# Two half-filled weight blocks share one: the feed-forward stage of a layer with 16-head attention

## The reference

```
xn  = layernorm(x)                          # x: 2048 tokens x 256
att = softmax(q k^T / sqrt(128)) v          # 16 heads of 128, q, k, v from xn @ Wqkv.T
x1  = xn @ quant(w1).T                      # quant(w): each weight to -1, 0 or 1
x2  = xn @ quant(w2).T                      # 704 inner features
ffn = (sigmoid(x1) * x2) @ quant(w3).T      # 704 -> 256
out = x + att @ Wout.T + ffn
```

## Time and profile before

| | before |
|---|---|
| median of 3 runs | 1920.66 us (1920.07 to 1921.25) |
| the profiled execution | 1918.09 us |
| its span, first to last instruction | 1916.3 us |
| PE busy | 1873.7 us, 98% of the span, 9540 matmuls |
| DVE, POOL, ACT busy | 1648.0, 1352.1, 1253.9 us |
| mean granted PE clock | 0.996 of full |

### The profile page before, as it was taken

One profiled execution on the slowest core, in us unless ns is written; L12 is line 12 of the kernel. 1 busy time (PEld: TensorE's weight loads), 2 busy tenths in 40 slices (PEclk: granted clock), 3 DMA queues, 4 the chain that ended last, 5 costly groups with the idle time before them and its releaser, 6 DMA issues.

```text
span 1916.3 us, 29455 instructions
## 1 busy us (share of the span) xinstructions
PE 1873.7 (98%) x9540; PEld 1583.2 (83%) x9540; DVE 1648.0 (86%) x2216; ACT 1253.9 (65%) x1700; POOL 1352.1 (71%) x514
## 2 busy tenths in 40 slices
PE   5979999999999999999999999999999999999998
PEld 4868888888888888888888888888888888888887
DVE  6368898898989889898989989898998989889895
ACT  3437676766767676666767666676766667666664
POOL 2418687776868777686877768687776868777685
PEclk9999999999999999999999999999999999999999
DMA  3037677676767767676776767677676767767664
GB/s 106 0 81 174 156 171 171 156 170 158 173 156 173 172 151 172 158 170 157 174 170 152 171 158 170 158 173 171 152 170 158 169 159 170 174 147 168 156 159 128
DMA packets 195827, 298.59 MB, mean 156 GB/s; under 512 B 37888, under 2 KB 57024, under 8 KB 195776
## 3 DMA queue, kind: packets, MB, share of 16 engines
q1 hardware_dynamic: 195776, 298.01, 66.5%
HBM read 12.65 MB, written 2.10 MB: 8 GB/s over the span
## 4 chain that ended last, share of the span: by engine, by line
PE 90%; DVE 3%; SPq 2%; POOL 2%; ACT 1%; issue 1%; DMA 1%; DVEq 0%; POOLq 0%; ACTq 0%
PE ps_o L375 23%; PE ps_o L377 12%; PE ps_s L367 11%; PE ps_s L369 11%; PE ps_s L368 11%; PE ps_s L338 5%; PE ps_t L357 4%; PE ps_t L347 4%; SPq L284 2%; PE ps_s L410 2%; PE ps_o L385 1%; PE ps_o L387 1%; PE ps_o L386 1%; POOL parts L1044 1%; DVE prob L896 1%
## 5 line engine op out<-in xcount | busy, mean ns | idle before, releaser
L1044 POOL TENSOR_TENSOR parts<-raw,parts 128x2048 fp32r<-128x2048 f32 x254 | 1176.8, 4634 | 446.0 <-ACT parts L674 445.1
L686 ACT ACTIVATE prob<-ps_s,neg_max 128x1024 f32<-128x1024 f32 x512 | 567.4, 1115 | 470.9 <-DVE neg_max L890 470.9
L375 PE MATMUL ps_o<-parts,v_hi 128*128 128x512 f32 x2032 | 728.7, 397 | 2.6 <-POOL v_lo L1037 2.6
L886 DVE TENSOR_REDUCE row_max<-ps_s 128x1 f32<-128x1024 f32 x512 | 612.2, 1213 | 68.8 <-PE ps_s L369 49.5
L896 DVE STREAM_TRANSPOSE prob<-prob 128x1024 f32<-128x1024 f32 x508 | 599.5, 1218 | 57.6 <-ACT prob L686 57.2
L377 PE MATMUL ps_o<-parts,v_lo 128*128 128x256 f32 x2032 | 571.2, 281 | 0.0
L674 ACT CAST parts<-raw 128x2048 fp32r<-128x2048 f32 x254 | 486.7, 1916 | 87.9 <-DMA raw<-prob 86.7
L375 PEld LDWEIGHTS ps_o<-parts,v_hi 128*128 128x128 f32 x2032 | 382.3, 188 | 91.3 <-issue 3.9
L367 PE MATMUL ps_s<-k_hi,q_hi 128*128 128x512 f32 x1024 | 404.7, 395 | 11.6 <-ACT prob L686 11.0
L369 PE MATMUL ps_s<-k_hi,q_lo 128*128 128x512 f32 x1024 | 400.8, 391 | 0.0
L368 PE MATMUL ps_s<-k_lo,q_hi 128*128 128x512 f32 x1024 | 400.3, 391 | 0.0
(11 more groups left out here) (113 smaller groups left out, 1630.2 us busy)
## 6 DMA issues: line engine op xcount, KB each, us to landing
raw<-prob SPq DMA_DIRECT2D x2032, 128.0 KB, 2.4
v_raw<-v_turned SPq DMA_DIRECT2D x244, 64.0 KB, 2.0
w_raw<-wqkv_dram SPq DMA_DIRECT2D x32, 128.0 KB, 2.5
y<-x_dram SPq DMA_DIRECT2D x4, 512.0 KB, 6.0
wo_raw<-wqkv_dram SPq DMA_DIRECT2D x16, 128.0 KB, 2.5
wo_raw<-wo_dram SPq DMA_DIRECT2D x16, 128.0 KB, 2.3
out_dram<-y SPq DMA_DIRECT2D x8, 256.0 KB, 2.7
w_raw<-w_dram SPq DMA_DIRECT2D x2, 704.0 KB, 10.6
```

The source lines that it names most:

```text
L375: nc.tensor.matmul(ps_pv, v_hi[:, kb, :], parts[:, kb].rearrange("p s a q -> p (s a q)"), start=(kb == 0), stop=False, skip_group_check=True)
L686: nc.scalar.activation(tile, logit, ACT.Exp, bias=neg_max[:, t:t + 1], scale=SCALE, accum_out=row_sum[:, t, half:half + 1]).then_inc(s_exp, 1)
L886: nc.vector.reduce_max(row_max[:, t, half:half + 1], ps_s[:, 2 * half:2 * half + 2, :].rearrange("p b n -> p (b n)"), AX_X).then_inc(s_mx, 1)
L1044: nc.gpsimd.tensor_tensor(half_of(0, half), moved(p, half), half_of(1, half), ALU.subtract).then_inc(s_pl, 1)
```

## The change

The last block of w1 (64 columns) and the last block of w2 (64 columns) are put into one block of `w1_q`. One set of 4 matmuls then gives x1's last 64 features on partitions 0 to 63 and x2's on 64 to 127 of one bank. ACT's sigmoid reads partitions 0 to 63 and writes 64 to 127, and DVE multiplies there. The high part stays on partitions 64 to 127 of `hid_hi`'s last block; the low part is now made by DVE and written to partitions 0 to 63 of the same block, and POOL's loop has five blocks. The last 64 rows of w3 are loaded a second time, beneath the first copy, so that one matmul for each tile multiplies high and low part together. The second load overwrites the zeros that the mean of w3 needs, and waits for that mean.

```diff
             w1_q = sb("w1_q", [P, C, FB * P], F32R, early)
-            w2_q = sb("w2_q", [P, C, FB * P], F32R, early)
+            w2_q = sb("w2_q", [P, C, FL], F32R, early)
...
-            hid_lo = sb("hid_lo", [P, FB, CH], F32R, early)
+            hid_lo = sb("hid_lo", [P, FB - 1, CH], F32R, early)
...
                 load_part(part, 0)
+            sp.wait_ge(s_abs, 3)
+            sp.dma_start(w3_raw[FR:P, FB - 1, :], w3_d[FL:FF, :]).then_inc(s_w3_again, 16)
...
-                for w, k in ((w1_q, 0), (w2_q, 1)):
+                for w, k in ((w1_q, 0), (w2_q, 1))[:1 if b == FB - 1 else 2]:
...
             def ffn_down(g):
                 for b in range(FB):
-                    pe.wait_ge(s_hidl, g * FB + b + 1)
+                    if b < FB - 1:
+                        pe.wait_ge(s_hidl, g * (FB - 1) + b + 1)
+                    else:
+                        pe.wait_ge(s_hidlast, g + 1)
                     for j in range(TG):
                         dst = (ps_t if j < 2 else ps_o)[:, j % 2, 0:DIM]
-                        nc.tensor.matmul(dst, hid_hi[:, b, j * P:(j + 1) * P], w3_q[:, b, :],
-                                         start=(b == 0), stop=False)
-                        last = nc.tensor.matmul(dst, hid_lo[:, b, j * P:(j + 1) * P], w3_q[:, b, :],
-                                                start=False, stop=(b == FB - 1))
+                        last = nc.tensor.matmul(dst, hid_hi[:, b, j * P:(j + 1) * P], w3_q[:, b, :],
+                                                start=(b == 0), stop=(b == FB - 1))
+                        if b < FB - 1:
+                            nc.tensor.matmul(dst, hid_lo[:, b, j * P:(j + 1) * P], w3_q[:, b, :],
+                                             start=False, stop=False)
...
             for b in range(FB):
+                if b == FB - 1:
+                    pe.wait_ge(s_wshared, 1)
                 ffn_up(0, b, b == 0)
...
-                nc.scalar.activation(sig[:, b % 2, :], ps_s[:, 2 * (b % 2), :], ACT.Sigmoid).then_inc(s_sig, 1)
+                n = FR if b == FB - 1 else P
+                nc.scalar.activation(sig[P - n:P, b % 2, :], ps_s[0:n, 2 * (b % 2), :], ACT.Sigmoid
+                                     ).then_inc(s_sig, 1)
...
-                nc.scalar.copy(hid_hi[:, b, :], hid[:, b % 2, :]).then_inc(s_hidh, 1)
+                n = FR if b == FB - 1 else P
+                nc.scalar.copy(hid_hi[P - n:P, b, :], hid[P - n:P, b % 2, :]).then_inc(s_hidh, 1)
...
-            quantise(1, w2_raw, w2_q[:, :, 0:FF])
+            quantise(1, w2_raw, w2_q[:], w1_q[:, :, FF:FB * P])
...
-                    dve.wait_ge(s_hidl, g * FB + b - 1)
-                nc.vector.tensor_tensor(hid[:, b % 2, :], ps_s[:, 2 * (b % 2) + 1, :], sig[:, b % 2, :],
+                    dve.wait_ge(s_hidl, g * (FB - 1) + b - 1)
+                n, bank = (FR, 2 * (b % 2)) if b == FB - 1 else (P, 2 * (b % 2) + 1)
+                nc.vector.tensor_tensor(hid[P - n:P, b % 2, :], ps_s[P - n:P, bank, :], sig[P - n:P, b % 2, :],
                                         ALU.mult).then_inc(s_hid, 1)
...
             def add_ffn(g):
+                dve.wait_ge(s_hidh, g * FB + FB)
+                nc.vector.tensor_tensor(hid_hi[0:FR, FB - 1, :], hid[FR:P, (FB - 1) % 2, :], hid_hi[FR:P, FB - 1, :],
+                                        ALU.subtract).then_inc(s_hidlast, 1)
                 dve.wait_ge(s_down, g + 1)
...
                     dve.wait_ge(s_gamma, 6)
+                    dve.wait_ge(s_w3_again, 16)
                     quantise(2, w3_raw, w3_q[:])
...
-            nc.gpsimd.memset(w1_q[:, :, FF:FB * P].bitcast(F32), 0.0).then_inc(s_pads, 1)
-            nc.gpsimd.memset(w2_q[:, :, FF:FB * P].bitcast(F32), 0.0).then_inc(s_pads, 1)
...
-                for b in range(FB):
+                for b in range(FB - 1):
```

More of the change, by code:

```diff
@@ L39 @@
 FR = FF - (FB - 1) * P
+FL = FF - FR
 G = 4
@@ L191, in build @@
         s_wq = sem("quantised_weights_ready")
+        s_wshared = sem("shared_block_ready")
+        s_w3_again = sem("w3_last_rows_loaded_again")
         s_ln = sem("layernorm_step_done")
@@ L202, in build @@
         s_hidl = sem("hidden_low_ready")
+        s_hidlast = sem("hidden_last_low_ready")
         s_down = sem("ffn_down_done")
@@ L815, in thresholds, with quantise @@
                                         ).then_inc(s_gamma, 1)
-            def quantise(i, raw, q):
+            def quantise(i, raw, q, shared=None):
                 n = raw.shape[1] * raw.shape[2]
@@ L821, in quantise @@
                     dve.wait_ge(s_wq, i)
+                if i == 2:
+                    dve.wait_ge(s_wshared, 1)
                 nc.vector.tensor_scalar(is_below, raw[:], half_gamma[:, 1, i:i + 1], None, ALU.is_lt
@@ L824, in quantise @@
                 dve.wait_ge(s_below, i + 1)
-                nc.vector.scalar_tensor_tensor(out=q, in0=raw[:], scalar=half_gamma[:, 0, i:i + 1], in1=is_below,
-                                               op0=ALU.is_gt, op1=ALU.subtract).then_inc(s_wq, 1)
+                n = raw.shape[2] if shared is None else FL
+                nc.vector.scalar_tensor_tensor(out=q, in0=raw[:, :, 0:n], scalar=half_gamma[:, 0, i:i + 1],
+                                               in1=is_below[:, :, 0:n], op0=ALU.is_gt, op1=ALU.subtract
+                                               ).then_inc(s_wq, 1)
+                if shared is not None:
+                    nc.vector.scalar_tensor_tensor(out=shared, in0=raw[:, :, FL:FF],
+                                                   scalar=half_gamma[:, 0, i:i + 1], in1=is_below[:, :, FL:FF],
+                                                   op0=ALU.is_gt, op1=ALU.subtract).then_inc(s_wshared, 1)
             normalise(0)
@@ L1004, in _ @@
             nc.gpsimd.memset(ident[:], 0.0).then_inc(s_pads, 1)
-            nc.gpsimd.memset(w1_q[:, :, FF:FB * P].bitcast(F32), 0.0).then_inc(s_pads, 1)
-            nc.gpsimd.memset(w2_q[:, :, FF:FB * P].bitcast(F32), 0.0).then_inc(s_pads, 1)
-            pool.wait_ge(s_pads, 3)
+            pool.wait_ge(s_pads, 1)
             nc.gpsimd.memset(w3_raw[FR:P, FB - 1, :], 0.0).then_inc(s_w3_pad, 1)
@@ L1010, in _ @@
             nc.gpsimd.memset(ones[:], 1.0).then_inc(s_pads, 1)
-            pool.wait_ge(s_pads, 4)
+            pool.wait_ge(s_pads, 2)
             nc.gpsimd.affine_select(out=ident[:], in_=ident[:], compare_op=ALU.not_equal, fill=1.0, base=0,
```

## The result

| | before | changed |
|---|---|---|
| median of 6 runs each, on the same chip | 1919.3 us (1917.29 to 1921.25) | 1912.47 us (1910.85 to 1915.14) |
| ratio, 95% interval | | 0.9966 (0.9954 to 0.9978) |
| the profiled execution | 1918.09 us | 1913.44 us |

A forecast was written before the change was run, and what follows sets the result against it. PE, busy for 98% of the span, was taken to bound the kernel. Removed work, added instructions and clock, -4.66 + 0.19 + 0.3 = -4.2 us, off the median 1920.66 gave 1916.5 us, range 1914.7 to 1918.2.

The forecast's parts named there:

- Groups 1 to 3: Feed-forward groups without PE waits: each loses 4 up and 4 down matmuls, 1.39 us, 4.18 us for three.
- The up matmuls of group 0: Ahead of the wait for w3: their 0.92 us gain nothing, PE waits 3.3 us instead of 2.4.
- The sixth block: Last block of the down-projection: its low part from DVE arrives in time, margin 0.8 us, so no cost.
- DVE's second instruction: Quantising w2 becomes two DVE instructions; the normalising behind starts some 0.06 us later, and that goes on the path.
- The clock, +0.3 us: Group 0's down-projection behind the w3 wait: longer idle brings more of the lower clock rate, 0.3 us lost.
- rival B: Group 0's first 11 down matmuls run slow too, costing 1.03 us: gain 3.4 us, 1917.2 us; chance 0.20.
- The registers, +0.13 us: Down-projection loop on PE: 12 more register and sequencer instructions over three groups, 0.011 us each, 0.13 us added.
- The attention is left as it is and only begins earlier: The over 1800 us behind the feed-forward stage: unchanged in length, only starting earlier.
- heads of a changed length: Attention: heads whose length has changed would show the forecast wrong; no size given.
- The level: Whole kernel: the 4.2 us gain taken off the runs' median, 1920.66 us, 2.6 us above the profiled execution: 1916.5 us.
- C: Group 0's slow clock stretch vanishes or falls into the gap: gain 6.0 us, 1914.7 us; chance 0.12.
- rival E: Sixth down block: moving between partition halves makes the serial chain 2.5 times as long, 5.7 us slower, 1926.4 us; chance 0.03.

The follow-up runs named there:

- the down part alone: Kernel before with only the down-projection's last block shared, 4 matmuls in place of 8, up-weights in separate zero-padded blocks; 1914.88 us, ratio 0.9983.
- the longer chain: Changed kernel with four more unused DVE subtractions, one behind the other, ahead of the one making the last low part; 1920.76 us, ratio 1.001.
- halves twice: Changed kernel with the last step of quantising w3 in two halves, behind blocks 3 and 4; 1910.64 us, and 1911.06 us when run again.
- the comparison on POOL: The version with w3 quantised in two halves, with the comparison that begins it moved from DVE to POOL; 1911.82 us, ratio 0.9965.
- the padded kernel: Changed kernel with 14 transposes of the identity added at the start of PE's program, result overwritten; 1912.74 us, ratio 0.9971.
- its up part: Kernel before with only the last blocks of w1 and w2 shared; the down-projection keeps 8 matmuls for its last block; 1914.44 us, ratio 0.998.

## Why the prediction missed

**Right, by its own steps.** Groups 1 to 3 lost 4.19 us (forecast 4.18): a matmul's price taken from the distance of starts, times the matmuls left out. That it is right to 0.01 us is luck, as the down part alone missed by 0.3. The up matmuls of group 0 were worth nothing, with the wait at 3.2 us (forecast 3.3). The sixth block came with 0.85 us to spare (0.8), and the extra subtractions measured that cover directly. The new row took 0.69 us, the lower of the two bounds. From the end of the x loads to group 1, the kernel gained 0.35 us (forecast 0.475 less the 0.06 of DVE's second instruction). That instruction took 0.81 us, not the 0.24 of the forecast; at most 0.07 us of it beyond the forecast reached PE.

**The clock, +0.3 us: wrong.** The slow stretch was the same. The term took "more idle can only bring more of the slow level", and rival B that a slow start costs 1.03 us more. Of the fourteen traces, eleven have a slow stretch in group 0's down-projection, behind gaps of 2.2 to 3.25 us. It begins anywhere from the first matmul (the longer chain, the down part alone) to 1.4 us behind it and ends some 3.4 us later. The eight of these traces that have 44 down matmuls need 6.52 to 6.60 us for them, first start to last pair; the three without it (halves twice, the comparison on POOL) need 5.03 to 5.09. So the price was 1.5 us or nothing, and neither the gap nor the slow start moved it. **The registers, +0.13 us: wrong.** They cost nothing that the groups' 15.3 us show. Together these two took some 0.4 us off the forecast gain.

**"The attention is left as it is and only begins earlier": the step that failed.** It begins 4.9 us earlier (first key matmul at 95.7 instead of 100.6), 0.7 more than the sum says: 0.3 from the transfers of x, 8.15 us instead of 8.47 in these traces (7.11 to 8.57 over all, for no reason found), and the 0.4 us above. The prediction had named heads of a changed length as a sign of being wrong, and there they are: head 14 is 1.4 us shorter, which the padded kernel ties to PE's program, and head 1 is longer by 0.1 to 1.2 us, by the pair of traces (111.59 and 112.26 us before, 112.32 to 112.75 in the changed kernel), which was not followed up. In the two traces first shown all this comes to 4.7 us of span, 1916.3 against 1911.6, 0.5 over the sum. The other 2.1 us of the 6.8 lie between the medians and the traced executions. A head 0 that is 3.3 us longer, in one of the two traces of the kernel before and in none of the three of the changed one, has the right size for that; the share of executions that have it was not measured.

**The level: wrong.** The profiled executions alone would have been forecast well: 1918.09 - 4.2 = 1913.9 us, and 1913.44 was measured. The prediction took the difference off the median of three, 1920.66. All three lay in the upper group of the six, so their median was no level for the kernel; that the 2.6 us between them and the profiled execution are a long head 0 is likely, but none of the three was traced. The median of all six, 1919.3, and those of the later sets, 1918.45, 1918.4 and 1917.85, lie 1.4 to 2.8 us lower. Of the 4.0 us between 1916.5 and 1912.47, the level explains 1.4 and the larger gain 2.6; the later sets put that gain at 5.3 to 6.2 us, so 1.1 to 2.0 us over the sum.

Of the rivals, none describes what happened. C's gain of 6.0 us has the right size by accident: its slow stretch in group 0 stayed.

## What to carry to other kernels

Where an engine is fed without a gap, count what is removed and multiply by the distance of two starts; that was good to 0.01 us in 4.2 for the whole change, to 0.1 us for its up part and to 0.3 us for its down part. Before taking such a sum off a median, look at how the single executions lie: if the profiled one stands apart from the rest, find out what differs in it, and give the forecast for each kind. Where the clock may fall behind a gap, count the slow stretch as there or not there, and don't scale it with the gap. And after a change to a program, compare also the stretches that were not touched.

## What the runs showed of the hardware

- **Moving between halves of the partitions is free here.** DVE's subtraction from partitions 64 to 127 to 0 to 63 takes 0.69 us, and so does the same subtraction in the up version, which stays within 64 to 127. ACT's sigmoid from 0 to 63 to 64 to 127 takes 0.59 us, and 0.60 on all 128 partitions in place. The Trainium skill (Vector Engine (DVE) Microarchitecture Reference, "3.8 The reshape front-end and per-opcode configuration") says that an instruction on 33 to 64 partitions may write to either half and can't straddle them. The trace agrees that the other half may be written. The page gives no duration for it; it is the row that speaks against rival E's slower chain.
- **DVE and POOL block each other.** In group 0 the new subtraction started at 44.95, beside POOL's, and took 1.15 us. POOL's ended 0.55 us before DVE's:

```profile
44.27 1.28 POOL L1059 TENSOR_TENSOR hid_lo<-hid,hid_hi 128x512 fp32r<-128x512 f32 x1 [2.94 <-ACT hid_hi L633]
```

```profile
44.95 1.15 DVE L874 TENSOR_TENSOR hid_hi<-hid,hid_hi 64x512 fp32r<-64x512 f32 x1 [0.68 <-ACT hid_hi L633]
```

The small second instruction for w2 took 0.81 us instead of the 0.24 forecast, and ended 0.15 us after POOL's row that ran to 25.05; the half of w3 took 1.90 us instead of 1.00 and ended 0.8 us after POOL's. The Trainium skill (SBUF — State Buffer, "Who interferes with whom") has a DVE instruction with two SBUF inputs contend with a GpSimd one that reads SBUF, and the ports that the two share are an exclusive lock. The trace agrees: each time DVE's row is longer than alone and ends behind POOL's. The comparison moved to POOL shows a dearer case, in which DVE's instructions have one tensor as input: 4.79 us for 1.37 us of DVE's work, from 30.04 to 34.83, beside POOL rows from 28.61 to 32.77 and from 32.99 to 34.36.
- **The clock after a gap.** After a gap of 1.9 us in the kernel with the longer chain the lower rate came at once behind one wait, 1.3 us later behind another, and not at all behind the third. In group 0 it came 0 to 1.4 us behind gaps of 2.2 to 3.25 us, and in the halves version, after 2.4 us, not at all. Where it came, it lasted some 3.4 us, which costs 1.5 us.
- **A DMA issue on SP can depend on PE's program.** One issue of 16 takes 2.1 us instead of 0.6 in head 14, the first behind the loop, when PE's program is 14 instructions longer. How the one reaches the other is open.
